# Moving the squares of the layer norm from ScalarE to GpSimd, and two layer-norm blocks and eight loads to the start, in a macaron transformer layer

## The reference

```python
def _layernorm(x, axis=-1, eps=1e-5):
    m = jnp.mean(x, axis=axis, keepdims=True)
    v = jnp.var(x, axis=axis, keepdims=True)
    return (x - m) / jnp.sqrt(v + eps)

# ffn: h = x W1^T + scale * x m1^T + b1; gelu; h W2^T + scale * h m2^T + b2
# (m1, m2 are outer products of a few tokens of x), hidden width 4096
# attn: xn = x / |x| * sqrt(1024) * gamma; q, k, v; causal softmax, 8 heads of 128; output matrix
x = x + 0.5 * ffn(_layernorm(x))
x = x + attn(_layernorm(x))
x = x + 0.5 * ffn(_layernorm(x))
```

## Time and profile before

| | |
|---|---|
| median of the two runs | 5101.91 us (4897.78 and 5306.04) |
| the profiled execution's own time | 4900.76 us |
| its span (core 1, the slowest) | 4899.2 us |
| spans of the other cores | 4870.8 to 4893.9 us |
| mean granted TensorE clock, all cores | 0.867 to 0.872 of full speed |
| PE busy | 3772.9 us, 77% of the span |
| ACT busy | 1297.4 us, 26% |
| DVE busy | 747.4 us, 15% |
| POOL busy | 63.7 us, 1% |

### The profile page before, as it was taken

The page is one execution under the profiler, slowest core; times in us unless marked ns, Lnnn a source line. Parts: engine busy times, 40 slices in busy tenths (PEclk is TensorE's granted clock), DMA queues, the critical chain, the costliest instruction groups (busy, mean ns, idle before and its releaser), DMA issues.

```text
span 4899.2 us, 43989 instructions; the slowest of 8 cores (4870.8 to 4899.2 us)
## 1 busy us (share of the span) xinstructions
PE 3772.9 (77%) x14584; PEld 1308.9 (27%) x14584; DVE 747.4 (15%) x1209; ACT 1297.4 (26%) x2031; POOL 63.7 (1%) x114
## 2 busy tenths in 40 slices
PE   3068799767887864978969869976788776497997
PEld 0023234222232211333323323422223221133333
DVE  2000200431131123001010020043113212300000
ACT  1022121214523531312212212121452353131221
POOL 0000000000000000001000000000000000000000
PEclk7579799888898886989989979988889788798998
DMA  9952233210100100235234223321010010023434
GB/s 192 209 123 68 64 86 99 62 40 18 42 11 16 31 16 13 61 93 140 64 107 127 63 62 94 93 63 50 16 41 14 16 31 16 12 60 97 112 80 129
DMA packets 437189, 334.32 MB, mean 68 GB/s; under 512 B 321198, under 2 KB 325680, under 8 KB 436972
## 3 DMA queue, kind: packets, MB, share of 16 engines
q1 hardware_dynamic: 394612, 252.00, 19.3%
q0 software_dynamic: 18144, 50.34, 5.2%
q10 hardware_dynamic: 24216, 29.18, 2.1%
HBM read 314.12 MB, written 42.46 MB: 73 GB/s over the span
## 4 chain that ended last, share of the span: by engine, by line
PE 65%; DMA 14%; DVE 7%; ACT 7%; issue 6%; ACTq 1%; DVEq 0%; SPq 0%; POOL 0%; POOLq 0%
PE ps L754 19%; PE ps L823 17%; PE ps L970 4%; PE ps L765 3%; PE ps L1041 3%; PE ps L1051 3%; PE ps L1143 2%; PE ps L791 2%; PE ps L1018 2%; PE ps L941 2%; DMA arena<-w2T 2%; DMA rep_a<-browL 1%; ACT f32t L844 1%; DMA wb<-w2s 1%; DMA browF<-srow_a 1%
## 5 line engine op out<-in xcount | busy, mean ns | idle before, releaser
L754 PE MATMUL ps<-xn,wb 128*128 128x512 bf16 x4096 | 987.6, 385 | 160.9 <-DMA wb<-w1s 141.8
L823 PE MATMUL ps<-arena,wb 128*128 128x512 bf16 x4096 | 896.6, 380 | 33.9 <-ACT u L800 23.2
L772 ACT ACTIVATE arena<-ps,b1c 128x512 bf16<-128x512 f32 x512 | 351.3, 687 | 714.5 <-PE ps L765 702.3
L823 PEld LDWEIGHTS ps<-arena,wb 128*128 128x128 bf16 x4096 | 396.9, 98 | 532.7 <-issue 68.3
L754 PEld LDWEIGHTS ps<-xn,wb 128*128 128x128 bf16 x4096 | 361.7, 98 | 653.3 <-issue 297.7
L1028 ACT ACTIVATE pb<-ps,negm 128x512 bf16<-128x512 f32 x640 | 419.3, 686 | 231.9 <-PE ps L1018 141.4
L852 DVE SCALAR_TENSOR_TENSOR R<-f32t,R 128x512 f32<-128x512 f32 x128 | 88.6, 692 | 2434.7 <-ACT f32t L844 1699.0
L844 ACT ACTIVATE f32t<-ps,b2c 128x512 f32<-128x512 f32 x128 | 88.0, 687 | 1001.7 <-PE ps L837 900.7
L1041 PE MATMUL ps<-pb,onesc 128*1 128x512 bf16 x640 | 263.1, 411 | 85.5 <-ACT pb L1028 85.4
L1018 PE MATMUL ps<-arena 128*128 128x512 bf16 x640 | 264.8, 423 | 31.5 <-ACT pb L1028 31.5
L1051 PE MATMUL ps<-pb,arena 128*128 128x512 bf16 x640 | 271.1, 424 | 4.0 <-DVE arena L1079 4.0
(11 more groups left out here) (87 smaller groups left out, 1872.9 us busy)
## 6 DMA issues: line engine op xcount, KB each, us to landing
wb<-w2s SPq DMA_DIRECT2D x512, 256.0 KB, 2.6
wb<-w1s SPq DMA_DIRECT2D x256, 256.0 KB, 3.0
f32t<-browF ACTq DMA_DIRECT2D x64, 256.0 KB
outT<-R POOLq DMA_DIRECT2D x64, 256.0 KB, 3.6
arena<-w1T POOLq DMA_DIRECT2D x4, 2048.0 KB, 27.9
w1s<-arena SPq DMA_DIRECT2D x4, 2048.0 KB, 14.5
arena<-w2T POOLq DMA_DIRECT2D x4, 2048.0 KB, 36.2
w2s<-arena SPq DMA_DIRECT2D x4, 2048.0 KB, 16.7
```

Of the source, the lines that this page charges most:

```text
L754: t_mm = p.emit("pe", lambda e, cc=cc, n0=n0, wt=wt, bank=bank: e.matmul(bank[:, :], wt[:, cc * 128:(cc + 1) * 128], xsl(cc, n0), start=(c ...
L772: t_g = p.emit("act", lambda e, hc=hc, nh=nh, bank=bank: e.activation(h_act(hc, nh), bank[:, :], AF.Gelu, bias=b1c[:, hc:hc + 1]), deps=[t ...
L823: t_mm = p.emit("pe", lambda e, oc=oc, hc=hc, nh=nh, wt=wt, bank=bank: e.matmul(bank[:, :], wt[:, oc * 128:(oc + 1) * 128], h_act(hc, nh), ...
```

## The change

Three edits. The squares of `ln_block` get a parameter `sq_eng`: with "act" they are the old ACT instruction, with "pool" a product of the slice with itself on POOL. All calls in the hooks ask for "pool". The two blocks of tile 1 in the first net of the first sequence leave the hook and are computed at the start, on ACT and with the spreading by matmul. And the eight loads that fill blocks 2 and 3 of `R` for the first sequence are issued on SP ahead of the stores of W1 instead of behind them.

```diff
         def ln_block(n0, gamma_fused, bcast_pe=False, sq_eng="act"):
...
-                    t_sq = p.emit("act", lambda e, cc=cc, n0=n0, pr=pr: e.activation(
-                        sqt[:, pr * 512:(pr + 1) * 512], rsl(cc, n0), AF.Square),
+                    if sq_eng == "act":
+                        sqf = lambda e, cc=cc, n0=n0, pr=pr: e.activation(
+                            sqt[:, pr * 512:(pr + 1) * 512], rsl(cc, n0), AF.Square)
+                    else:
+                        sqf = lambda e, cc=cc, n0=n0, pr=pr: e.tensor_mul(
+                            sqt[:, pr * 512:(pr + 1) * 512], rsl(cc, n0), rsl(cc, n0))
+                    t_sq = p.emit(sq_eng, sqf,
                         deps=B("R").deps_read(rslot(cc, n0)) + B("sqt").deps_write(pr), tag="sq")
...
                     layer_norm(t0, NT, False, bcast_pe=prologue_pe_bcast)
+                if ti == 0 and prologue_pe_bcast:
+                    layer_norm(NT, NT, False, bcast_pe=True)
...
         load_R_blocks(0, 1, 2)
+        load_R_blocks(0, 2, 4)
         emit_prep([b for b in _blocks if b[0] == "w1"])
-        load_R_blocks(0, 2, 4)
         emit_prep([b for b in _blocks if b[0] != "w1"])
...
                     if ti == 0 and nh == 0:
-                        ln_block(NT, False)
-                        ln_block(NT + 512, False)
+                        if not first:
+                            ln_block(NT, False, sq_eng='pool')
+                            ln_block(NT + 512, False, sq_eng='pool')
                         t1_compute(NT)
...
                         if ti == 0 and nh == 1:
-                            ln_block(0, False)
+                            ln_block(0, False, sq_eng='pool')
                         elif ti == 1 and nh == 0:
-                            ln_block(512, False)
+                            ln_block(512, False, sq_eng='pool')
```

More of the change, by code:

```diff
@@ L464, in next_w, with layer_norm, ln_block @@
             return _wbs[i]
-        def layer_norm(t0, ntok, gamma_fused, bcast_pe=False):
+        def layer_norm(t0, ntok, gamma_fused, bcast_pe=False, sq_eng="act"):
             for n0 in range(t0, t0 + ntok, 512):
-                ln_block(n0, gamma_fused, bcast_pe)
-        def ln_block(n0, gamma_fused, bcast_pe=False):
+                ln_block(n0, gamma_fused, bcast_pe, sq_eng)
+        def ln_block(n0, gamma_fused, bcast_pe=False, sq_eng="act"):
             if True:
@@ L1193, in ffn1_hook @@
                     if ti == 0 and nh == 0:
-                        ln_block(NT, False)
-                        ln_block(NT + 512, False)
+                        if not first:
+                            ln_block(NT, False, sq_eng='pool')
+                            ln_block(NT + 512, False, sq_eng='pool')
                         t1_compute(NT)
                     elif ti == 1 and nh == 0:
-                        ln_block(0, True)
-                        ln_block(512, True)
-                        ln_block(NT, True)
+                        ln_block(0, True, sq_eng='pool')
+                        ln_block(512, True, sq_eng='pool')
+                        ln_block(NT, True, sq_eng='pool')
                     elif ti == 1 and nh == 1:
-                        ln_block(NT + 512, True)
+                        ln_block(NT + 512, True, sq_eng='pool')
                 ffn(hook=ffn1_hook, ln_pre=(1,) if first else (0, 1),
```

## The result

The changed kernel took 5085.87 us, the median of 11 runs (4945.32 to 5296.3); the kernel before, in runs beside them, 5035.25 us, the median of 10 (4897.78 to 5306.72). In many executions of both kernels the cores of one die, sometimes of both, show a lower granted clock than the rest (0.77 to 0.85 against 0.87) and end later, so here and in every experiment only executions without it are compared, and where there is none, only the unaffected die. Compared so, the ratio is 1.0104, 95% interval 1.008 to 1.0129: the change costs about 51 us. The compared times of the changed kernel are 4945.32 to 4955.97 us; the profiled one is 4952.86 us, with a span of 4951.3.

A forecast was written before the change was run, and what follows sets the result against it. PE's own order of work and its standstills were taken as the bound. Terms -53.6 + 2 + 36.8 + 0.5 - 1.6 + 37.3 + 37.7 + 16 = +75 on 4900.76 gave 4976 us, range 4915 to 5045.

The forecast's parts named there:

- The moved blocks, -53.6: First hook: two blocks leave its 67.93 us, 14.35 remain; at the start they fit PE's 141.78 us idle time.
- The loads of `R`, +2: Start, SP queue: loads passing W1's stores cost 2 us, near the case of full DMA engines.
- Length of a POOL square: All POOL squares: time S of one square, taken as 1.35 us between bounds of 0.69 and 2.08.
- open blocks: Eight blocks where ACT has nothing in hand: 6S + 1.3 = 9.4 us against 4.8, +36.8 in all.
- A term put at nothing: Whole run: forecast starts from the profiled 4900.76 us and adds nothing for what lifted the other run.
- POOL's queue, +37.3 and +37.7: Second net's two hooks: squares queue behind 16 DMA issues, PE waits; 3.5 us come back at each.
- Exclusion, 16: Two- and three-block hooks: 36 POOL squares disturb DVE's pairs; 16 us, a third of the full 49.
- The rival of 49 us: DVE's pairs in two- and three-block hooks: POOL and DVE fully exclude each other, 5009 us; chance 0.2.
- Covered blocks, -1.6: Three hooks behind the adds, ACT still busy: 9.4 us on POOL against 9.95, so -1.6 in all.
- long squares: Rival, squares on the path: S = 2.08, 69 us more, 5045 us; chance 0.08.
- no stall in the queue: Rival: squares were what PE waited for and POOL's queue holds nothing up, 4744 us; chance 0.04.
- Short squares: Rival: S = 0.69 and no disturbance, 62 + 16 us less, 4898 us, no loss; chance 0.13.

The follow-up runs named there:

- experiment 4: Changed kernel with all squares on ACT and the eight loads of R back behind the stores of W1: ratio 0.9879 to the kernel before.
- experiments 1 and 2: Against the changed kernel: first, second net's two hook blocks back on ACT, 0.9972 of before; second, squares stay on POOL, next sequence's loads behind the hook, 4872.92 us.
- experiment 6: Changed kernel with the second and third blocks of the first nets' three-block hooks back on ACT: ratio 1.0092 to the kernel before.

## Where the prediction went wrong, and where it was right

*The moved blocks, -53.6.* Right: -54.1 and -54.4. The twin hook of the earlier trace rows priced what is left, and PE's idle time at the start covered the rest, as experiment 4 shows.

*The loads of `R`, +2.* Right within what can be seen. The profiled execution's +10.1 is scatter of the start. I had not put such scatter into the range, though every hook's gain is read behind it.

*Length of a POOL square.* This is the term of the sum that failed: "I take 1.35, about the middle and nearly two DVE rows". It is 1.04, one and a half DVE rows. On the 94 squares of the path 0.31 us each are 29 us by the prediction's own sum. By place 21 of them can be read: open blocks 25.5 for 36.8, the third attention hooks -4 for +0.5, and 2.5 in each of the two hooks behind the queue. That is the larger part of the 24 to 40 us between +75 and the measured 35 to 51. I had written 1.0 as the low end of the range, so the range held it. The factor of the Trainium skill (GPSIMD Engine Reference, section 3) and the middle of my bounds happened to meet at 1.35, and that agreement was no second piece of evidence. The mechanism beside it (PE follows POOL in 6S + 1.3, and what is late behind it moves along) was right: 7.5 by the sum with the true S, 7.7 measured.

*A term put at nothing.* "I forecast nothing of what lifted the other" of the two runs, 5306.04 us for 4897.78: the range held only executions like the profiled one. Half of all runs of the changed kernel took 5085.87 us or more, above its upper end of 5045. The kernel before shows the same (a median of 5035.25), so it is no effect of the change, and no run here shows what brings it about.

*POOL's queue, +37.3 and +37.7.* The mechanism was right, and experiments 1 and 2 show it from both sides. The size was too large: 29 to 31 and 25. With S at 1.04, 8 squares take 2.5 us less in each hook. The 16 DMAs took 5 and 8 us less by the medians of cores: I took over their length from a trace in which PE, ACT and DVE were busy beside them. Together that is 7 and 10 us, where 6 to 8 and 12 were missing.

*Exclusion, 16.* Near in size, and by luck: a third of an upper bound was taken because no row spoke for more. Measured are 11 to 12 us in the three-block hooks and none that shows in the two-block hook. The count of 36 squares was wrong: a touched DVE instruction costs 0.3 to 0.9 us, and in the three-block hook shown 14 were touched, 8 of them among its 48 pair instructions, 8.8 us in all. The rival of 49 us had the mechanism and not the number, since POOL's squares are done when most of the pairs begin.

*Covered blocks, -1.6.* With the true S this would have been about -7. In experiment 6, which takes the exclusion off the later blocks, the two three-block hooks end at about +1 and -2 against before, so little of it arrived; the adds and the row that the first block's squares stretch stand in its way.

*What else.* 3 to 8 us lie scattered over stages that I costed at nothing, single ones up to 3.6 either way, and I have no cause for them.

The rivals: long squares (2.08) and no stall in the queue are refuted by rows above. Short squares (0.69) came nearest of them, half way: S is 1.04, and its end at no loss did not come.

## What to carry to other kernels

Before work is moved to an idle engine, read what stands ahead of it in that engine's queue at each place: DMA issues that wait for other DMAs make an idle engine a late one, and here 16 squares of 160 cost more than all the others. When a slow producer feeds PE in open places, look at how many results it may have ready before PE comes: six buffers in place of two were worth 36 us at the same engine and speed. And price such a move by place, block by block, since neither the share of busy time nor the sum of waits told which blocks would gain.

## What the runs showed of the hardware

- A product of a 128x512 float32 slice with itself into bf16 takes 1.04 us on POOL, and 8 in a row take 8.06 (0.692 us is DVE's row for two float32 inputs, 0.622 ACT's square).
- DVE instructions with two inputs in SBUF and POOL's squares stretch each other: DVE from 0.75 to 1.34 us and from 0.69 to 1.56, down to a row of one partition (0.67 to 1.52), and POOL from 8.06 to 9.90 us for eight. The adds of the attention, which have one operand in SBUF and one in PSUM, kept their length (0.69 us) under POOL's squares.
- Eight pairs of a 256 KB store and the load that waits for it took 37.5 to 48.0 us in POOL's queue, 4.7 to 6.0 us a pair; stores alone went out every 1.6 us, as fast as DVE made the chunks.
- The start, where the DMA share is near 1, differs by some 7 us either way between executions (281.7 to 295.8 us to the first W1 matmul in 11 of them; 295.8 and 283.1 for the same kernel).
